# A graph layer on one Trainium2 core: edge attributes split ahead of the edge loop, and a bias row written into PSUM by VectorE and ScalarE

## What is computed

```python
edge_feat = concatenate([x[src], x[dst], edge_attr], axis=-1)   # 20000 x (512 + 512 + 64)
h = mish(edge_feat @ W1 + b1)                                    # first edge layer
messages = mish(h @ W2 + b2)                                     # second edge layer
agg = segment_sum(messages, dst, num_segments=1250)
u = mish(concatenate([x, agg], axis=-1) @ W3 + b3)
out = u @ W4 + b4
```

## Time and profile before

| what | value |
|---|---|
| median of three runs | 1122.53 us |
| span of the profiled execution, first to last instruction | 1119.2 us |
| PE busy | 1066.3 us (95%) |
| ACT busy | 889.8 us (80%) |
| DVE busy | 863.1 us (77%) |
| POOL busy | 661.0 us (59%) |
| mean granted TensorE clock | 0.988 of full speed |

### The profile page before, as it was taken

The page is one execution under the profiler, slowest core; times in us unless marked ns, Lnnn a source line. Parts: engine busy times, 40 slices in busy tenths (PEclk is TensorE's granted clock), DMA queues, the critical chain, the costliest instruction groups (busy, mean ns, idle before and its releaser), DMA issues.

```text
span 1119.2 us, 18504 instructions
## 1 busy us (share of the span) xinstructions
PE 1066.3 (95%) x5756; PEld 900.7 (80%) x5757; DVE 863.1 (77%) x1506; ACT 889.8 (80%) x1122; POOL 661.0 (59%) x558
## 2 busy tenths in 40 slices
PE   3768999999999999999999999999999999999997
PEld 1226889998888888888888888888888888888796
DVE  7998435526335588888899989998988888888786
ACT  6985736525504899999999999999999999999584
POOL 6874340002156576676888888888867677660217
PEclk9969999999999999999999999999999999999999
DMA  2005720301265486666666666666666666651002
GB/s 104 8 1 138 127 76 1 123 1 57 86 216 116 104 188 140 141 130 137 139 134 136 136 139 137 132 132 143 133 140 131 138 140 135 136 127 43 1 1 92
DMA packets 61087, 121.41 MB, mean 108 GB/s; under 512 B 7851, under 2 KB 18348, under 8 KB 60918
## 3 DMA queue, kind: packets, MB, share of 16 engines
q0 software_dynamic: 38048, 87.58, 38.3%
q1 hardware_dynamic: 22998, 33.32, 8.9%
HBM read 107.82 MB, written 7.80 MB: 103 GB/s over the span
## 4 chain that ended last, share of the span: by engine, by line
PE 88%; DVE 7%; issue 2%; ACT 2%; POOL 1%; DVEq 1%; ACTq 0%; POOLq 0%
PE banks L1072 12%; PE banks L1067 12%; PE banks L1068 12%; PE banks L970 10%; PE banks L1052 7%; PE banks L1092 6%; PE banks L1046 6%; PE banks L1013 5%; PE banks L888 4%; PE banks L1034 4%; PE banks L1065 3%; PE banks L1153 2%; DVE edge_counts L1737 2%; PE banks L818 1%; DVE key_onehot L1676 1%
## 5 line engine op out<-in xcount | busy, mean ns | idle before, releaser
L701 POOL DMA_INDIRECT gather_pq<-q_table,dst x157 | 296.0, 1885 | 57.1 <-issue 47.5
L693 POOL DMA_INDIRECT gather_pq<-p_table,src x157 | 172.9, 1101 | 136.7 <-PE banks L1052 83.6
L1067 PE MATMUL banks<-w_lo,h_hi 128*128 128x512 f32 x620 | 241.6, 390 | 0.0
L1068 PE MATMUL banks<-w_hi,h_hi 128*128 128x512 f32 x620 | 241.4, 389 | 0.0
L1072 PE MATMUL banks<-w_hi,h_lo 128*128 128x512 f32 x620 | 166.2, 390 | 0.0
L1068 PEld LDWEIGHTS banks<-w_hi,h_hi 128*128 128x128 f32 x620 | 116.4, 188 | 24.9
L1072 PEld LDWEIGHTS banks<-w_hi,h_lo 128*128 128x128 f32 x620 | 116.4, 188 | 24.2
L2050 DVE SCALAR_TENSOR_TENSOR h_full<-mish_work,banks 128x512 f32<-128x512 f32 (+1 forms) x154 | 98.5, 681 | 46.5 <-ACT mish_work L1377 42.1
L1067 PEld LDWEIGHTS banks<-w_lo,h_hi 128*128 128x128 f32 x620 | 116.5, 188 | 22.0
L2075 DVE SCALAR_TENSOR_TENSOR message<-mish_work,banks 128x1024 f32<-128x1024 f32 x78 | 95.3, 1222 | 8.7 <-ACT mish_work L1401 0.7
L1365 ACT ACTIVATE mish_work<-banks 128x1024 f32<-128x1024 f32 (+1 forms) x77 | 78.6, 1021 | 26.3 <-PE banks L1052 26.2
(11 more groups left out here) (270 smaller groups left out, 2671.5 us busy)
## 6 DMA issues: line engine op xcount, KB each, us to landing
edge_attr<-in_edge_attr_t SPq DMA_DIRECT2D x79, 128.0 KB
x_nodes<-h_hi POOLq DMA_DIRECT2D x10, 256.0 KB, 13.3
x_nodes<-h_lo POOLq DMA_DIRECT2D x10, 256.0 KB, 7.9
p_table<-p_stage SPq DMA_DIRECT2D x10, 256.0 KB, 2.0
q_table<-agg_nodes SPq DMA_DIRECT2D x10, 256.0 KB
gather_pq<-p_table,src POOLq DMA_INDIRECT x157
gather_pq<-q_table,dst POOLq DMA_INDIRECT x157
x_nodes<-in_x SPq DMA_DIRECT2D x3, 768.0 KB, 6.3
```

The lines of the kernel that those rows point to most:

```text
L693: nc.gpsimd.indirect_dma_start(GP[:, 2 * j + k, :], None, p_tab[:, :], bass.IndirectOffsetOnAxis(ap=SRC[:, 2 * s + k:2 * s + k + 1], axis= ...
L701: nc.gpsimd.indirect_dma_start(GP[:, 2 * j + k, :], None, q_tab[:, :], bass.IndirectOffsetOnAxis(ap=DST[:, 2 * s + k:2 * s + k + 1], axis= ...
L1067: pe.matmul(at, h_high(s, j)[:, c, e], W2_LO[:, c, :], start=False, stop=False)
L1068: pe.matmul(at, h_high(s, j)[:, c, e], W2_HI[:, c, :], start=False, stop=False)
```

## The change

It does two things.

First, the attributes are split ahead of the edge loop. The host stores each row once. In a new piece of POOL's program, between the clearing of the strip (L677) and the wait for `bn_ready` (L679), `attr_parts` runs 40 times: two steps' attributes (64 partitions each) are cast and subtracted at 128 x 256. SP loads the raw blocks and stores the high and the low parts to a DRAM table `attr_parts`, with 4 stores of 64 partitions and one load for each of the 40. SP does the first 20 of them ahead of its wait for MM_2 and the loads of ROWS and W1, and the other 20 between these loads and its wait for MM_PQ. In the edge loop SP loads a finished 128 x 256 block into one of 4 slots; `attr_high` and `attr_rest` are gone.

Second, from step 2 on PE's bias product is gone from `z2`, and the accumulation continues on a bank that holds b2 already. VectorE copies b2 (128 x 512) into the bank of tile 0 behind `hots1`, ScalarE into the bank of tile 1 between `sq2` and `log2`. PE waits for these copies.

```diff
+ATTR_BREAK = 20
...
+        AT_RAW, _ = sb("edge_attr", [P, 2, PW])
+        B2_ROW, _ = sb("b2_row", [P, 1, DIM], at=place[0] - 4 * 2 * PW)
+        AT_HI, _ = sb("edge_attr_hi", [P, 2, PW], F32R)
+        AT_LO, _ = sb("edge_attr_lo", [P, 2, PW], F32R)
...
-        AT_RAW, at = sb("edge_attr", [P, 2, PW], at=at)
-        AT_R, at = sb("edge_attr_parts", [P, 2, PW], F32R, at=at)
+        AT_R, at = sb("edge_attr_parts", [P, SLOTS, PW], F32R, at=at)
...
+        at_tab = nc.dram_tensor("attr_parts", [PAIRS, P, PW], F32)
...
+            def load_raw(n, j):
+                sp.dma_start(AT_RAW[:, j, :], edge_attr_t[bass.ds(2 * n, 2), :, :].rearrange("o p e -> (o p) e")).then_inc(attr_raw[j], 16)
+            def store_parts(n, j):
+                for done, part, rows in ((attr_hi, AT_HI, slice(0, EDGE_DIM)), (attr_lo, AT_LO, slice(EDGE_DIM, P))):
+                    sp.wait_ge(done, n + 1)
+                    for k in range(2):
+                        sp.dma_start(at_tab[bass.ds(2 * n + k, 1), rows, :].rearrange("o p e -> (o p) e"),
+                                     part[EDGE_DIM * k:EDGE_DIM * (k + 1), j, :].bitcast(F32)).then_inc(attr_stored[j], 16)
+            def split_pairs(first, end):
+                with sp.Fori(first // 2, end // 2) as i:
+                    for j in range(2):
+                        store_parts(2 * i + j, j)
+                        load_raw(2 * i + 2 + j, j)
+            for j in range(2):
+                load_raw(j, j)
+            split_pairs(0, ATTR_BREAK)
             sp.wait_ge(mm_done, MM_2)
             sp.dma_start(ROWS[:, :, :], rows.partition_broadcast(P)).then_inc(rows_in, 16)
             sp.dma_start(WA[:, :, :], w1[0:2 * DIM, :].rearrange("(k p) n -> p k n", p=P)).then_inc(w1_in, 16)
+            split_pairs(ATTR_BREAK, PAIRS // 2 - 2)
+            for j in range(2):
+                store_parts(PAIRS // 2 - 2 + j, j)
+            sp.dma_start(B2_ROW[:, :, :], rows[ROW_B2:ROW_B2 + 1, :].partition_broadcast(P)).then_inc(b2_in, 16)
...
-                sp.dma_start(AT_RAW[:, j, :], edge_attr_t[j, :, :]).then_inc(attr_in[j], 16)
+                sp.wait_ge(attr_stored[j], 16 * PAIRS)
+            def attributes(s, j):
+                sp.dma_start(AT_R[:, j, :].bitcast(F32), at_tab[bass.ds(s, 1), :, :].rearrange("o p e -> (o p) e")).then_inc(attr_in[j], 16)
+            for s in range(SLOTS):
+                attributes(s, s)
...
-            def attributes(i, pairs=2):
-                for j in range(pairs):
-                    sp.wait_ge(attr_ready, 2 * i + j - 1)
-                    sp.dma_start(AT_RAW[:, j, :], edge_attr_t[bass.ds(2 * i + j, 1), :, :]
-                                 .rearrange("o p e -> (o p) e")).then_inc(attr_in[j], 16)
-            attributes(1)
+            def further_attributes(s, j):
+                sp.wait_ge(z1_done, s - SLOTS + 1)
+                attributes(s, j)
             sp.wait_ge(mm_done, MM_U)
-            with sp.Fori(2, 2 + KD) as i:
-                attributes(i)
-                sp.dma_start(WB[:, bass.ds(i - 2, 1), :].rearrange("p o n -> p (o n)"),
-                             w3[bass.ds(DIM + (i - 2) * P, P), :]).then_inc(w3_in, 16)
-            with sp.Fori(2 + KD, EDGE_PAIRS // 2) as i:
-                attributes(i)
-            attributes(EDGE_PAIRS // 2, EDGE_PAIRS % 2)
+            with sp.Fori(1, 1 + KD) as i:
+                for j in range(SLOTS):
+                    further_attributes(SLOTS * i + j, j)
+                sp.dma_start(WB[:, bass.ds(i - 1, 1), :].rearrange("p o n -> p (o n)"),
+                             w3[bass.ds(DIM + (i - 1) * P, P), :]).then_inc(w3_in, 16)
+            with sp.Fori(1 + KD, EDGE_PAIRS // SLOTS) as i:
+                for j in range(SLOTS):
+                    further_attributes(SLOTS * i + j, j)
+            for s in range(EDGE_PAIRS // SLOTS * SLOTS, EDGE_PAIRS):
+                further_attributes(s, s % SLOTS)
...
+            def attr_parts(n):
+                j = n % 2
+                pool.wait_ge(attr_raw[j], 16 * (n // 2 + 1))
+                if n >= 2:
+                    pool.wait_ge(attr_stored[j], 64 * (n // 2))
+                nc.gpsimd.tensor_copy(AT_HI[:, j, :], AT_RAW[:, j, :]).then_inc(attr_hi, 1)
+                pool.wait_ge(attr_hi, n + 1)
+                nc.gpsimd.tensor_tensor(AT_LO[:, j, :], AT_RAW[:, j, :], AT_HI[:, j, :].bitcast(F32), ALU.subtract).then_inc(attr_lo, 1)
+            for n in range(PAIRS // 2):
+                attr_parts(n)
...
-                    pe.wait_ge(attr_ready, s + 1)
+                    if b == 0:
+                        pe.wait_ge(attr_in[slot], loaded)
                     for c in (2 * b, 2 * b + 1):
                         for w in (WE_HI, WE_LO):
-                            mm = pe.matmul(Z1v[:, c, 0:P * tiles(s)], w[:, c * P:(c + 1) * P], AT_R[:, j, 0:P * tiles(s)],
+                            mm = pe.matmul(Z1v[:, c, 0:P * tiles(s)], w[:, c * P:(c + 1) * P], AT_R[:, slot, 0:P * tiles(s)],
...
-                    if after(s, 2):
-                        pe.wait_ge(msg_full, s - 1)
-                    else:
+                    if not after(s, 2):
                         pe.wait_ge(up_moved, BLOCKS * KD)
                     pe.wait_ge(h_hi, s + 1)
-                pe.matmul(at, ONES_R[:, :], B2_R[:, :], start=True, stop=False)
+                if after(s, 2):
+                    pe.wait_ge((b2_first, b2_second)[k], s - 1)
+                else:
+                    pe.matmul(at, ONES_R[:, :], B2_R[:, :], start=True, stop=False, skip_group_check=True)
...
-            def attr_high(s, j, loaded):
-                act.wait_ge(attr_in[j], loaded)
-                if after(s, 2):
-                    act.wait_ge(z1_done, s - 1)
-                nc.scalar.copy(AT_R[:, j, :], AT_RAW[:, j, :]).then_inc(attr_hi, 1)
...
+            def b2_second_tile(s, j):
+                nc.scalar.copy(Z2[:, 2 * j + 1, :], B2_ROW[:, 0, :]).then_inc(b2_second, 1)
...
+                if after(s, 3) and live(s - 1) and tiles(s - 1) == 2:
+                    b2_second_tile(s - 1, 1 - j)
+                if live(s - 2):
                     log2(s - 2)
-                if live(s + 2):
-                    attr_high(s + 2, j, loaded)
...
-            def attr_rest(s, j):
-                dve.wait_ge(attr_hi, s + 1)
-                low = AT_R[EDGE_DIM:P, j, :]
-                nc.vector.tensor_tensor(low, AT_RAW[EDGE_DIM:P, j, :], low.bitcast(F32), ALU.subtract).then_inc(attr_ready, 1)
...
+            def b2_first_tile(s, j):
+                dve.wait_ge(msg_full, s - 1)
+                nc.vector.tensor_copy(Z2[:, 2 * j, :], B2_ROW[:, 0, :]).then_inc(b2_first, 1)
...
-                if live(s + 2):
-                    attr_rest(s + 2, j)
                 if live(s - 2):
                     hots1(s - 2, j)
+                    if live(s):
+                        b2_first_tile(s, j)
...
-        "edge_attr_t": np.concatenate([attr, attr], axis=1),
+        "edge_attr_t": attr,
```

More of the change, by code:

```diff
@@ L400, in gnn_kernel @@
         q_moved, p_stored, q_stored = sem("q_moved"), sem("p_stored"), sem("q_stored")
-        attr_in = [sem(f"attr_in{j}") for j in range(2)]
-        attr_hi, attr_ready = sem("attr_hi"), sem("attr_ready")
+        attr_raw = [sem(f"attr_raw{j}") for j in range(2)]
+        attr_stored = [sem(f"attr_stored{j}") for j in range(2)]
+        attr_in = [sem(f"attr_in{j}") for j in range(SLOTS)]
+        attr_hi, attr_lo = sem("attr_hi"), sem("attr_lo")
         z1_done, a_exp, a_sq, a_ln, a_r, h_hi, h_lo = (sem(n) for n in
@@ L406, in gnn_kernel @@
         h_full = [sem(f"h_full_{h}") for h in range(2)]
-        z2_done = sem("z2_done")
+        z2_done, b2_in, b2_first, b2_second = (sem(n) for n in ("z2_done", "b2_row_in", "b2_in_first_tile", "b2_in_second_tile"))
         b_exp, b_sq, b_ln, b_r, msg_full, msg_hi, msg_lo = (sem(n) for n in
@@ L1036, in u_terms, with z1 @@
                 mm.then_inc(mm_done, 1)
-            def z1(s, slot, j, gathered):
+            def z1(s, slot, gathered, loaded):
                 pe.wait_ge(gat1[slot], gathered)
@@ L1071, in z2 @@
                 for c in range(KD):
-                    mm = pe.matmul(at, h_low(s, j)[:, c, e], W2_HI[:, c, :], start=False, stop=(c == KD - 1))
+                    mm = pe.matmul(at, h_low(s, j)[:, c, e], W2_HI[:, c, :], start=False, stop=(c == KD - 1), skip_group_check=True)
                 if k == tiles(s) - 1:
@@ L1098, in extras1, with edge_step @@
                             FINAL_ROWS if final else MSG_ROWS)
[L1100 removed]
+            def edge_step(s, slot, gathered, loaded, group):
                 j = slot % 2
@@ L1105, in edge_step @@
                 if live(s):
-                    z1(s, slot, j, gathered)
+                    z1(s, slot, gathered, loaded)
                 if live(s - 2) and tiles(s - 2) == 2:
@@ L1421, in edge_step @@
                     sq2(s - 2)
+                if after(s, 3) and live(s - 1) and tiles(s - 1) == 2:
```

(20 more changed lines are left out.)

14 lines of the change are left out of this document (7 added, 7 removed).

## The result

The changed kernel takes 1155.11 us (median of four runs, 1153.58 to 1156.01); beside it on the same chip the kernel before took 1122.08. The ratio is 1.0295, 95% interval 1.0275 to 1.0314: slower, where I forecast 1110. The profiled execution's span is 1154.1 us, 34.9 more than before.

What follows compares the result with a forecast made beforehand. PE bounds the loop before, ACT after: -13.1 us in the loop, -0.9 behind it, +0.2 for first steps, +1.0 beside POOL, -12.8 against the 1119.2 span; 1106.4 plus 3.3 gives about 1110 us, range 1102 to 1124.

Steps and rivals of the forecast that it cites:

- What bounds the loop: Edge loop: PE bounds it before at 8.67 us a step, ACT after at 8.47; step taken as 8.49.
- the second half of the saving: Edge loop: PE saves 0.46 us a step, to 8.21, but ACT's cycle of 8.47 leaves more than half uncollected.
- DVE as the bound: Rival, edge loop: with a copy of 0.7 us DVE needs 8.63 a step, 1120 us in all; chance 0.16.
- cost 0: Before the second layer: POOL free at 268 us, needed only by 269.1, so the split delays nothing.
- ahead of the loop, POOL: Before the second layer: POOL's 40 casts and subtractions, 36 us of work in a 96.04 us gap, 2.3 us each.
- A buffer's hand-over: Split ahead of the loop: a buffer is free when its stores have landed; 4.1 us for two, 2.05 each.
- the bound of 3.0: Upper bound of the split's pace, with stores at 575 ns: 4 x 0.65 + 0.41 = 3.0 us, POOL free at 295 to 299.
- the stop at W1: Split ahead of the loop: loads of ROWS and W1 hold up the stores behind them once, taken as 7 us.
- SP's stores are slow: Rival, SP's queue before the second layer's tables: pace 3.0, POOL 26 to 30 us late, 1137 us; chance 0.14.
- four bias products: Behind the last full step, still on PE's path: 4 x 0.23 = 0.9 us saved.
- Beside POOL: DVE's five hidden_low beside POOL's work ahead of the loop: +1.0 us, between 0 and 3.1.
- From span to median: Whole kernel: the median stands 3.3 us above the profiled span, added to 1106.4 to give 1109.7.

## Why the prediction was wrong

- **What bounds the loop: right.** PE before, ACT after. A step of 8.47 (I took 8.49), -14.4 us in the loop (-13.1). The copies took 0.59 and 0.69 us (0.61 and 0.60). That the second half of the saving would not be collected was right, and two runs show that it can be had by giving ScalarE half as many copies.
- **DVE as the bound: did not happen,** though the copy took the 0.7 us that this rival asked for. Its only idle time in the loop of the changed kernel, 30.8 us in 32 waits between 460 and 1000 us, is ahead of full1, for ACT.
- **The step that failed is "cost 0" under "ahead of the loop, POOL".** It rests on a pace of 2.3 us a split, worked out from five DMAs of 0.33; the pace was 3.5. The only rows of 64-partition DMAs in the trace of before said 575 ns, and I kept them for the bound alone, "against" being that they stood behind a load of 1 MB and that all other single DMAs took about 0.33. The latter wasn't so either: the four loads of W02 took 0.40 to 0.47. The stores took 0.47 and, with what stands between two, 0.67. A buffer's hand-over, which I had worked out at 2.05, did not come into it. My 0.65 for them in the upper bound was close by luck: 0.57 for the issue was too much, and 0.08 between two too little. What was missing there was the register work around the load and the jump of SP's loop, and so the bound of 3.0 was itself 0.5 short. 172 + 39 x 3.5 + 9 for the stop at W1 (I took 7) makes 318, and POOL got free at 319.
- **The rival had the place right and the size wrong.** "SP's stores are slow" was given 0.14 and 1137 us. At a pace of 3.5 the P table is 49.8 us late, not 27.
- **One term was missing:** while PE waits its clock falls, and the stretch behind the wait took 2 us longer (116.9 against 114.9).
- **Smaller terms.** POOL's cast and subtraction took 1.14 us (0.40 and 0.74) where halves of longer ones had given 0.91. Behind the loop I had taken off 0.9 us for four bias products; from the sum that ends the 73 steps to the end it is 94.96 us before and 94.9 after, so next to nothing of it came.
- **Beside POOL: right,** as far as VectorE's own time goes: 1.33 us where I took 1.0. The rule of the Trainium skill, SBUF — State Buffer, Who interferes with whom, would have given 3. Five instructions of 1.42 us beside POOL's casts and subtractions lost 0.27 each on average, and POOL's cast of 0.40 took up to 1.66 there, so the blocking goes both ways, and it cost DVE less than one whole POOL instruction each.
- **The Trainium skill's tip that PSUM is ScalarE's faster destination** (ScalarE: Activation LUTs, Step-by-step: what each stage is for) changed nothing that shows: the copy took 0.59, and the columns' cost from SBUF rows had given 0.61.
- **From span to median:** 1.0 us here (1154.1 and 1155.1), where I had added 3.3. Every execution on record took 1.8 to 2.1 us more than its own span; the rest of the 3.3 was the spread between executions.
- **With stores of 128 partitions the forecast holds:** POOL free at 267.6 (268), the table at 273.8 and 275.4 (274 to 276), 1106 us (1110). That POOL's time fits to 0.4 us is luck: the pace was 2.07 us over the last 15 splits and not 2.3, the stop at W1 cost 10 and not 7, and the splits beside hidden_low lost another 3.6. Nor was there any slack: in both runs with one engine's copy alone PE waited 1.1 us for W1_LO.

## What to carry to other kernels

Work that is moved off a full engine into a gap needs the gap on every engine that it passes: here POOL's 96 us were enough for 46 us of work, and SP's queue, with five DMAs and their register work for each piece, was not. Count a DMA on its queue by a row of its own shape plus the gap to the next one. When the only row of that shape is dearer than the rest, put it into the sum and not only into the bound. And where two engines are within 3% of each other, try shifting work between them in halves: here a copy at every second step was worth 7 us more than one at every step.

## What the runs showed of the hardware

- A DMA between SBUF and DRAM held SP for 0.33 us with 128 partitions (of 256 or of 128 columns) and for 0.47 with 64, as the stores of the split and as the loads of the edge loop (medians; with wide stores the loop's loads have 64 partitions and took 469 ns, in the changed kernel 128 and 333). The shape isn't all of it: the split's loads of 128 partitions took 0.35 us beside the wide stores and 0.42 beside the narrow ones, and the eight stores of 64 partitions in the run without splits, which stand in no loop, 0.53 to 0.60. Two that follow each other in a counted loop stand about 0.2 us further apart than that.
- VectorE's load of three registers from SBUF took 0.75 us in the kernels before and after (743 to 757 ns, 40 times each) and mostly 1.50 in the version with the attribute part alone, from the same place in its program. What doubles it stays open: it was 0.75 with ScalarE's copy alone, 0.74 to 1.52 (median 0.93) with the bias part alone, and 0.75 to 1.48 with the load moved.
- VectorE writes 128x512 into PSUM in 0.69 us and ScalarE in 0.59.
